# Four buffers instead of two for the last turned keys, and one copy of turned probabilities moved between two high parts

## The reference, cut to what matters

```python
x = x + L0(x, weight[adapter]);  x = x + L1(x, lora);  x = x + L2(x, lora)
q = rope(rmsnorm(x @ Wq.T));  k = rope(rmsnorm(x @ Wk.T));  v = x @ Wv.T     # 32 / 8 / 8 heads of 128
k_all = concat([k_cache[block_table], k]);  v_all = concat([v_cache[block_table], v])   # 512 + 32 keys
scores = where(valid, q @ k_all.T / sqrt(128), -1e30);  probs = softmax(scores)
x = x + (probs @ v_all) @ Wo.T
```

## Time and profile before

| | us |
|---|---|
| median of 3 runs (lowest, highest) | 2474.97 (2472.66, 2476.22) |
| the profiled execution | 2474.47 |
| its span in the trace | 2472.9 |
| PE busy in the span | 2411.7 |
| DVE busy | 1800.9 |
| ACT busy | 1588.8 |

### The profile page before, as it was taken

One profiled execution on the slowest core, in us unless ns is written; L12 is line 12 of the kernel. 1 busy time (PEld: TensorE's weight loads), 2 busy tenths in 40 slices (PEclk: granted clock), 3 DMA queues, 4 the chain that ended last, 5 costly groups with the idle time before them and its releaser, 6 DMA issues.

```text
span 2472.9 us, 55761 instructions
## 1 busy us (share of the span) xinstructions
PE 2411.7 (98%) x16326; PEld 2195.6 (89%) x16327; DVE 1800.9 (73%) x3708; ACT 1588.8 (64%) x3328; POOL 684.0 (28%) x930
## 2 busy tenths in 40 slices
PE   6799999999999989999999999999999999999999
PEld 4688788888888779999999999999999999788887
DVE  6455537899998988788888878888888888644443
ACT  3222337777777778888888888888888888311111
POOL 1222140000000034554554455455445444000000
PEclk9899999999999999999999999999999999999999
DMA  6532432333334388888888888888888887766664
GB/s 232 161 115 78 135 124 86 114 105 99 101 99 118 111 259 301 284 298 299 283 296 304 289 288 297 293 288 298 300 286 293 297 297 271 257 228 212 217 207 140
DMA packets 377285, 541.48 MB, mean 219 GB/s; under 512 B 49522, under 2 KB 263218, under 8 KB 374386
## 3 DMA queue, kind: packets, MB, share of 16 engines
q1 hardware_dynamic: 305074, 316.33, 40.1%
q0 software_dynamic: 70016, 221.30, 25.7%
q10 hardware_dynamic: 2112, 2.89, 0.4%
HBM read 442.06 MB, written 98.30 MB: 219 GB/s over the span
## 4 chain that ended last, share of the span: by engine, by line
PE 62%; DMA 1%; DVE 1%; ACT 0%; issue 0%; DVEq 0%; ACTq 0%
PE both_ps_o L1369 18%; PE both_ps_s L108 10%; PE both_ps_s L110 10%; PE both_ps_s L109 10%; PE both_ps_pt L1346 9%; PE both_ps_o L1372 5%; DMA out_w<-in_wo 1%; PE both_ps_s L1352 1%; PE both_ps_s L1354 0%; DMA k_own<-qkv_out_t 0%; DVE att_prob L1083 0%; DVE out_w_lo L1464 0%; ACT att_prob L1059 0%; DVE out_o_lo L1482 0%; DVE out_o L1478 0%
## 5 line engine op out<-in xcount | busy, mean ns | idle before, releaser
L1369 PE MATMUL both_ps_o<-att_pt,att_v 128*128 128x128 f32 x4096 | 540.0, 275 | 0.0
L1059 ACT ACTIVATE att_prob<-att_prob,att_shift 128x544 f32<-128x544 f32 x512 | 384.1, 750 | 206.4 <-DVE att_shift L1083 196.2
L1369 PEld LDWEIGHTS both_ps_o<-att_pt,att_v 128*128 128x128 f32 x4096 | 504.8, 191 | 0.0
L1083 DVE CUSTOM_DVE_ANT_0 att_prob<-both_ps_s,att_mask 128x544 f32<-128x544 f32 x512 | 366.2, 715 | 0.0
L1054 DVE TENSOR_TENSOR att_k_lo<-att_k_raw,att_k_hi 128x1024 fp32r<-128x1024 f32 (+1 forms) x320 | 338.4, 1058 | 1.9 <-ACT att_k_hi L1044 1.9
L108 PE MATMUL both_ps_s<-att_k_hi,att_q_hi 128*128 128x272 f32 x1024 | 338.3, 330 | 0.5 <-DVE att_k_lo L1054 0.5
L1167 POOL DMA_INDIRECT att_v<-in_v_pages,att_rows_now x256 | 289.9, 1132 | 85.1 <-issue 83.9
L1346 PE MATMUL both_ps_pt<-both_ident,att_prob 128*128 128x128 f32 x2048 | 307.8, 273 | 2.0 <-ACT att_pt L1243 2.0
L110 PE MATMUL both_ps_s<-att_k_hi,att_q_lo 128*128 128x272 f32 x1024 | 297.2, 290 | 0.0
L109 PE MATMUL both_ps_s<-att_k_lo,att_q_hi 128*128 128x272 f32 x1024 | 294.4, 288 | 0.0
L1243 ACT ACTIVATE att_pt<-both_ps_pt 128x512 f32<-128x512 f32 x512 | 294.3, 575 | 0.1
(11 more groups left out here) (195 smaller groups left out, 5150.0 us busy)
## 6 DMA issues: line engine op xcount, KB each, us to landing
att_k_raw<-in_k_pages SPq DMA_DIRECT2D x1024, 128.0 KB, 5.7
q_t<-qkv_out_t SPq DMA_DIRECT2D x128, 256.0 KB, 2.3
att_q_raw<-q_t POOLq DMA_DIRECT2D x64, 512.0 KB, 7.2
o_t<-att_o POOLq DMA_DIRECT2D x64, 512.0 KB, 6.6
out_o<-o_t SPq DMA_DIRECT2D x32, 1024.0 KB, 6.7
out_inv<-inv_t SPq DMA_DIRECT2D x32, 1024.0 KB, 7.1
qkv_w_stage<-in_w_qkv SPq DMA_DIRECT2D x12, 1024.0 KB, 5.2
early_stage<-in_w SPq DMA_DIRECT2D x10, 1024.0 KB, 7.3
```

What stands on the lines that cost most here:

```text
L1059: act.activation(prob[:, b, :], prob[:, b, :], ACT.Exp, bias=shift[:, b:b + 1], scale=-1.0, accum_out=total[:, j // HK, j % HK:j % HK + 1] ...
L1083: dve.tensor_tensor_reduce(out=prob[:, b, :].rearrange("p (a n) -> p a n", a=2), in0=ps_s[:, j % 2, :, 0:HALF], in1=mask[:, j // HK, :].re ...
L1369: pe.matmul(out, v_sb[p][:, c, h * DH:(h + 1) * DH], pt_sb[:, j % OG, c, :], start=(c == 0), stop=False)
```

## The change

The last four steps get an `out_last` buffer each, and none of them waits for a store. As four buffers reach over `q_lo` into `k_lo`, `lo_part` waits for all stores before each piece of sequence 1, not before the queries' piece alone. In the first six units of attention only the first of a unit's listed high parts comes before `copy_pt`, the others after; only unit 0 has two.

```diff
+OUT_LAST = 4
-    out_last = Region(nc, "qkv", place[1].first + AT_Q_LO).sb("out_last", [P, 2, SPT, 4, SEQ])
+    out_last = Region(nc, "qkv", place[1].first + AT_Q_LO).sb("out_last", [P, OUT_LAST, SPT, 4, SEQ])
     def is_late(n):
-        return isinstance(n, int) and n >= ALL_STEPS - 2
+        return isinstance(n, int) and n >= ALL_STEPS - OUT_LAST
+
+    def out_buffer(n, j):
+        return out_last[:, j % OUT_LAST, :, :, :] if is_late(n) else out_t[:, j % 2, :, :, :]
         def store(b, j, n, which, c):
-            out = out_last if is_late(n) else out_t
             sp.wait_ge(out_ready, n + 1)
-                         out[:, p, :, :, :].rearrange("p s h q -> p s (h q)")).then_inc(stored[p], 16)
+                         out_buffer(n, j).rearrange("p s h q -> p s (h q)")).then_inc(stored[p], 16)
             if later(n, 2) and not is_late(n):
                 act.wait_ge(stored[p], stores)
-            out = out_last if is_late(n) else out_t
-            act.activation(out[:, p, :, :, :], ps_t[p].rearrange("p h (s q) -> p s h q", s=SPT),
+            act.activation(out_buffer(n, j), ps_t[p].rearrange("p h (s q) -> p s h q", s=SPT),
                            ACT.Copy).then_inc(out_ready, 1)
     def lo_part(dve, s, p, c):
         dve.wait_ge(hi_done, turn)
-        if c == PIECE_Q and later(s, 1) and not later(s, 2):
+        if later(s, 1) and not later(s, 2):
             for n in range(2):
                 dve.wait_ge(both.stored[n], 16 * ALL_STEPS // 2)
                 if not later(u, EARLY):
-                    for c in FIRST_HI[j]:
+                    for c in FIRST_HI[j][:1]:
                         hi_part(act, 1, 1, 1, c)
...
                 copy_pt(u, j)
+                if not later(u, EARLY):
+                    for c in FIRST_HI[j][1:]:
+                        hi_part(act, 1, 1, 1, c)
```

## The result

The changed kernel takes 2479.49 us (median of 8 runs, 2478.5 to 2484.74), the kernel before 2473.97 (8 runs, 2471.92 to 2476.22): ratio 1.0025, interval 1.0016 to 1.0034, so 4 to 8 us slower. The forecast was 2478.4, in a range of 2473.2 to 2482.0. The time lies in the range, and the chain was the one described; but of the three classes the likeliest one, "the same", was missed by a little: +5.5 us stand against a bound of 5, which lies inside the interval, so that these runs don't decide between "the same" and "slower". The profiled execution took 2478.79 (span 2477.2), 4.3 more than that of before. It is one of the quicker of the eight.

What follows compares the result with a forecast made beforehand. PE bounds the kernel, busy 98% of the span, so the change counts by how far PE's steady run shifts. New wait +3.3 (including -0.6), more waits +0.1, clock and copy 0: +3.4 us, forecast 2478.4 us, range 2473.2 to 2482.0.

Steps and rivals of the forecast that it cites:

- the same: Class of outcome: time within 0.2% (5 us) of the kernel before; chance 0.74.
- Copy 28: ACT's copy of step 28 in the last block, no longer waiting for a store: 893.95 instead of 895.74, 1.79 us earlier.
- The last rotation: DVE's last rotation before the handover: still at 897.1, ending at 897.80, limiting the last turn's gain to 0.63 us.
- The first low part: DVE's first lo_part of sequence 1: waits for the last store, starts at 907.05 instead of 903.71, +3.3 us.
- the landing of the last store: Last store of turned keys: issued near 899.6, latency 7.3 us, landing near 906.95; ends 904.1 and 907.85.
- That credit: Last store's latency: 0.2 to 0.5 us taken off 7.6 because earlier stores use idle DMA time.
- What the load is: Late stores at the handover: latency laid to four value gathers on POOL's queue and sequence 2's key pages on SP's.
- The "-0.6": Handover: four buffers alone let the first low part start at 903.08 instead of 903.71; gain hidden by the new wait.
- The copy's place: Copy of turned probabilities between unit 0's high parts on ACT: cost 0, gain 0, under DVE's new wait.
- The clock: PE's granted clock after its waits at the handover: change taken as 0, ends -1.4 and +1.4 us.
- rival B: At the new wait, late landing and low clock together: +5.7 us, 2480.7; chance 0.16.
- The rule for a quicker landing: 2.0 us fixed plus bytes by 436 GB/s: 2.6 us per 256 KB store; supports stores landing in time, chance 0.20.

Runs made afterwards that it cites:

- e1: Kernel before with one line changed: lo_part waits for all stores before each low part of sequence 1; +5.9 us (+3.7 to +8.2) against before.
- e2: Four late buffers, the two more in memory cleared only after all stores land, old wait, old order on ACT; 0.0 us (-2.2 to +2.2) against before.
- e3: Changed kernel with the two more buffers elsewhere and the old wait, new order on ACT kept; -0.5 us (-2.7 to +1.7) against before.
- e6: Changed kernel with sequence 2's key pages held back until the first low part of sequence 1 is done; +5.2 us (+3.0 to +7.7) against before.
- e7: Changed kernel with key pages held back, and three of four value gathers held until all stores landed; +4.9 us (+2.5 to +7.2) against before.
- e4: Changed kernel with the old order on ACT, both high parts and then the copy; +5.4 us (+3.2 to +7.7) against before.
- e5: Kernel before with only the new order, copy of turned probabilities between unit 0's two high parts; -1.0 us (-3.2 to +1.2) against before.
- e9: Kernel before, unchanged, run again for a second trace; 18.76 us from the last rotation to the first scores of sequence 1.
- e10: Changed kernel, unaltered, run again for a second trace; 2481.51 us.
- e8: e3 with sequence 1's first piece a step earlier, high and low lists not moved equally; +2.7 us (+0.5 to +4.9) against before.
- e11: e3 with two pieces of sequence 1 early, high and low parts kept a unit apart; 2470.73 us, -4.5 us (-6.7 to -2.0) against before.

## Why the prediction was right, and where it was not

*Right, step by step.* Copy 28 was forecast at 893.95 and came at 894.05, without a wait. The last rotation stayed (897.22), so that the turn behind it gained 0.5 us where 0.63 was said. The first low part waited for the last store. PE then stood still for 5.0 us, from 904.7 to 909.7, where "904.3 to about 909" was said. The rest of the chain kept its length, B 12.80 against 12.59. e1 shows the new wait as the cause, and e2 and e3 show that without it nothing is lost, within 2.2 us.

*The term that was mis-sized* is the landing of the last store. I put 7.3 us of latency and 906.95; it took 7.8 from 899.75, and DVE went on at 907.71, 0.66 late. Against before the first low part moved by 4.0 instead of 3.3, and with 0.2 in B and 0.1 behind the attention that makes the 4.3 of the profiled executions. I had credited the earlier stores with 0.2 to 0.5 us by using idle DMA time. That credit is not to be seen: the last store took 7.8 and 8.4 us in the changed kernel, 7.6 and 8.6 in the kernel before. Nor could it be, for one kernel's two traces lie as far apart; one trace of before did not show that this term moves by a microsecond by itself.

*What the load is* was half wrong. The working named gathers and pages; e6 shows no part of the pages in it, e7 that holding back gathers too leaves 3.3. An average share of the engines was the wrong witness: it was 0.33 and then 0.04 in e6 while the store was still out. Which of the engines or what in them keeps the store is not settled; a trace by engine would be needed.

*The "-0.6"* was read as a fixed gain of the four buffers. It is there in one trace of before and not in the other. Up to 1.16 us (1.79 - 0.63) of the copy's wait is free, because DVE's rotation comes later anyway; with 1.69 us something is lost, with 0.95 nothing. That the changed kernel gave back little was in the forecast; that there may be nothing to give back was not.

*The copy's place* was put at 0, and e4 and e5 bear it out.

*The clock* was put at 0 with 1.4 either way. B has two parts. The first goes from the first low part to the matmul with which PE returns from its last wait for a maximum (909.41 before, 913.42 in the changed kernel); it is 5.7 to 5.8 us in the ten traces of the table. The second goes from there to the first scores of sequence 1, and its length follows the granted clock:

| traces | mean granted clock | second part of B, us |
|---|---|---|
| e2, e3 | 1.00 | 5.44, 5.57 |
| before, e9, e5 | 0.76 to 0.77 | 6.89 to 7.07 |
| changed, e10, e4 | 0.75 | 7.05 to 7.09 |
| e6, e1 | 0.66, 0.64 | 7.94, 8.15 |

The rows of e2, the changed kernel and e1 (1.00 is 2.4 GHz, and below it part of the stretch ran at 0.50, 1.2 GHz):

```profile
909.48:914.92 5.44, 4.94 (x41) 4.71 (x41) 5.22 (x11) 5.44 (x12) 4.35 (x8) 1.00 0.96 321
```

```profile
913.42:920.51 7.09, 6.59 (x42) 6.36 (x42) 5.36 (x11) 6.01 (x12) 6.17 (x7) 0.75 0.99 331
```

```profile
912.60:920.75 8.15, 7.65 (x42) 7.42 (x42) 5.37 (x11) 6.14 (x12) 6.24 (x7) 0.64 0.97 325
```

So the bounds were about right, and the chosen 0 fits the changed kernel (+0.2), but in part by luck. Its low stretch lasted from 906.8 to 917.0, against 909.1 to 912.6 before (3.4 us, where the forecast had 2.9, from a row that ends at 912), as rival B had feared; only 3.6 us of it fell into the part of B that the clock lengthens, against 3.1 before. In e1 and e6 it was 5.9 and 5.4. There the grant fell 0.7 and 1.1 us before the end of PE's long wait, in the changed kernel 2.9 and 3.0. The length of PE's wait does not sort them: 5.1 us in e1, 5.0 and 5.4 in the changed kernel. Why the grant falls when it does is open.

*Median against trace.* The sum was made for one execution (+3.4, measured +4.3), the medians differ by 5.5. A + B of both traces of each kernel gives 4.6 on average, inside the interval of 4 to 8. The last microsecond is not resolved by these runs.

*Luck in the level.* The forecast of 2478.4 stands on the median of three runs, 2474.97; over eight runs that kernel has 2473.97. So the time was missed by 1.1 us, but the difference by 2.1 (+3.4 against +5.5). The lower end of the range takes the spread of the runs as 1.3 us either way, though the lowest of them lay 2.3 below the median; nothing hangs on it here.

*The rule for a quicker landing.* The rule weighed in the forecast (2.6 us for such a store, from the Trainium skill, "DMA: Bandwidth & Descriptors", "Anatomy of one DMA — SWDGE (gpsimd) path") was rightly kept to a rival. Its section is on transfers issued from GpSimd and does not say that they must be alone, as I wrote; these stores are issued by SP. It comes near the 3.3 us of e7, where three gathers are held back, and is a third of what the changed kernel shows.

## What to carry to other kernels

Before more buffers are laid over memory that a later stage writes early, ask when the last of their transfers lands and what stands behind the write on its engine: here 1.7 us of stall on ACT were removed, of which 1.2 were free anyway, and DVE, the engine that sets the pace, stood idle for 6.3 us instead of 1.9 ahead of its first low part. The same buffers in memory whose next writer already waits for these transfers cost nothing (0.0 us, give or take 2.2). And where an engine idles at a handover, the distance between a producer's and a consumer's list must be kept when both move up: that is the difference between +2.7 us (e8) and -4.5 us (e11).

## What the runs showed of the hardware that was not expected

A 256 KB store took 2.3 us in the quiet stretch and 3.3 with three of the four gathers held back (e7). Behind all four gathers on another queue, the last store took 7.6 and 8.6 us in two traces of the kernel before, 7.8 and 8.4 in two of the changed kernel, and 8.9 in e6, there at a mean share of the DMA engines of 0.33 over two of its last three microseconds. The landing of one store can thus be late while the engines on average are mostly idle.
